# Dilated attention: another order of TensorE's work within a unit

## What is computed

```
qkv = einsum('bhwc,oc->bohw', x, Wqkv)          # q, k, v for 2 dilations (2 and 3), 64 channels each
kw, vw = unfold_windows(k, v, 3 x 3 taps, dilation)
attn = softmax(einsum('bndhw,bndkhw->bnkhw', q, kw) * 0.25, over the 9 taps)   # per head and position
out  = einsum('bnkhw,bndkhw->bndhw', attn, vw)
x    = x + concat(out) @ Wproj.T + bproj
```

## Time and profile before

| | |
|---|---|
| median of 3 runs | 7381.07 us (7369.02 to 7398.86) |
| profiled execution | 7399.85 us |
| its span, first to last instruction | 7397.9 us |
| mean granted clock of PE | 0.688 |
| PE busy | 3084.1 us, 42% |
| DVE busy | 3409.7 us, 46% |
| ACT busy | 1538.9 us, 21% |
| POOL busy | 2602.1 us, 35% |

### The profile page before, as it was taken

One profiled execution on the slowest core, in us unless ns is written; L12 is line 12 of the kernel. 1 busy time (PEld: TensorE's weight loads), 2 busy tenths in 40 slices (PEclk: granted clock), 3 DMA queues, 4 the chain that ended last, 5 costly groups with the idle time before them and its releaser, 6 DMA issues.

```text
span 7397.9 us, 84797 instructions
## 1 busy us (share of the span) xinstructions
PE 3084.1 (42%) x32140; PEld 1902.7 (26%) x32141; DVE 3409.7 (46%) x6941; ACT 1538.9 (21%) x3954; POOL 2602.1 (35%) x2472
## 2 busy tenths in 40 slices
PE   0011117687887798738874122222222222222205
PEld 0011106553773485226722000000000000000104
DVE  9999935757766685726665011111111111111128
ACT  0000005421651274016510011111111111111100
POOL 0000051100000000040001777777777777777450
PEclk9965558886997698658975555555565655555556
DMA  2000023000100100010002122222222222222207
GB/s 78 0 0 0 0 68 116 25 1 23 16 2 1 37 4 1 0 27 3 2 1 39 16 32 37 32 38 32 32 32 32 32 32 32 32 32 32 62 7 244
DMA packets 259708, 227.82 MB, mean 31 GB/s; under 512 B 115005, under 2 KB 222954, under 8 KB 250282
## 3 DMA queue, kind: packets, MB, share of 16 engines
q0 software_dynamic: 78944, 29.28, 6.3%
q1 hardware_dynamic: 99786, 99.91, 4.4%
q10 hardware_dynamic: 80640, 93.86, 4.1%
HBM read 100.42 MB, written 121.39 MB: 30 GB/s over the span
## 4 chain that ended last, share of the span: by engine, by line
PE 26%; another core or an unknown queue 23%; issue 18%; DVE 17%; DVEq 6%; ACT 4%; DMA 3%; POOL 2%; ACTq 1%; SPq 0%; POOLq 0%
DVE SA_ L1305 3%; PE PSB L382 2%; PE PSB L679 2%; DVE SA_ L1295 2%; PE PSB L1157 2%; PE PSB L661 2%; PE PSB L527 2%; PE PSB L352 2%; POOL VPAD L958 2%; DVEq L1386 1%; PE PSB L392 1%; DVE SA_ L583 1%; PE PSB L516 1%; PE PSB L366 1%
## 5 line engine op out<-in xcount | busy, mean ns | idle before, releaser
L948 POOL DMA_INDIRECT SA_<-s_T,GIX x2048 | 2186.6, 1068 | 659.0 <-issue 659.0
L1157 PE MATMUL PSB<-VPAD,EH 128*128 128x512 f32 x512 | 299.4, 748 | 1995.6 <-DMA VPAD<-s_TNT 1562.0
L940 POOL DMA_INDIRECT s_AEXP<-fill,SIX x128 | 139.2, 1087 | 2467.4 <-DMA fill<-s_ADT 2426.3
L897 DVE TENSOR_TENSOR XPAD<-SA_ 128x256 f32<-128x256 f32 x32 | 14.2, 444 | 1830.3 <-DMA SA_<-s_T,GIX 1830.3
L1157 PEld LDWEIGHTS PSB<-VPAD,EH 128*128 128x128 f32 x512 | 120.6, 245 | 2195.3 <-DMA VPAD<-s_TNT 1603.6
L1161 PE MATMUL PSB<-SA_,EW 128*128 128x512 f32 x512 | 346.3, 825 | 345.2 <-ACT SA_ L1142 198.6
L849 POOL DMA_INDIRECT SA_<-s_SK,BLKI x128 | 121.0, 945 | 1018.5 <-DVE BLKI L1438 976.9
L303 ACT ACTIVATE PRX<-PSB,MX 128x144 f32<-128x144 f32 x1024 | 375.3, 380 | 337.2 <-DVE MX L224 337.0
L1409 PE MATMUL PSB<-ident,SA_ 128*128 128x128 f32 x448 | 81.8, 364 | 838.0 <-DVE SA_ L1376 576.7
L1146 ACT ACTIVATE VPAD<-PSB,PRX 128x512 f32<-128x512 f32 x128 | 87.9, 687 | 1308.4 <-remote 941.7
L1142 ACT ACTIVATE SA_<-PSB,PRX 128x512 f32<-128x512 f32 x256 | 175.9, 687 | 773.7 <-remote 432.4
(11 more groups left out here) (365 smaller groups left out, 7536.3 us busy)
## 6 DMA issues: line engine op xcount, KB each, us to landing
SA_<-s_T,GIX POOLq DMA_INDIRECT x2048
s_Y<-VPAD ACTq DMA_DIRECT2D x32, 1024.0 KB
s_R<-zero SPq DMA_DIRECT2D x96, 256.0 KB
s_R<-XPAD ACTq DMA_DIRECT2D x32, 768.0 KB
SB_<-s_Y SPq DMA_DIRECT2D x16, 1024.0 KB, 5.4
SA_<-s_Y SPq DMA_DIRECT2D x16, 1024.0 KB, 7.3
s_AEXP<-zero SPq DMA_DIRECT2D x32, 256.0 KB, 3.0
SA_<-in_x SPq DMA_DIRECT2D x16, 512.0 KB
```

The costliest lines, as they stand in the source:

```text
L948: pool.indirect_dma_start(out=n.G[:,s,c,:],out_offset=None,in_=d["T"],in_offset=IOA(ap=n.GIX[s][:,c:c+1],axis=0)).then_inc(n.gath[s],16)
L1157: pe.matmul(PSB[:,(m%4)*512:(m%4+1)*512],n.WM1[:,m//2,(m%2)*P:(m%2+1)*P],n.TNC[:,s,:],start=True,stop=True).then_inc(n.moe_h,1)
```

## The change

In `l1conv_pe` the steps of a unit are put in another order. Before: head sums 0,1 of the next unit; expansions 0,1 and 2,3; the queries of the unit after the next; head sums 2,3 and 4,5; expansions 4,5; head sums 6,7,8. After: expansions 0,1; head sums 0,1; expansions 2,3; head sums 2,3; expansions 4,5; queries; head sums 4,5 and 6,7,8. The projection and expansions 6,7 and 8 follow as before. Nothing else is touched.

```
         turn_weights(m)
+        expand_pair(m,0)
         if more: logit_pair(m+1,0)
-        expand_pair(m,0); expand_pair(m,2)
+        expand_pair(m,2)
+        if more: logit_pair(m+1,2)
+        expand_pair(m,4)
         if m+2<UNITS: queries(m+2)
-        if more: logit_pair(m+1,2); logit_pair(m+1,4)
-        expand_pair(m,4)
+        if more: logit_pair(m+1,4)
         if more: logit_pair(m+1,6); logits(m+1,8)
         if closing: project(m//2-1,0)
         expand_pair(m,6)
```

## The result

| | before | after |
|---|---|---|
| median of 6 runs each | 7394.32 us (7369.02 to 7407.17) | 7452.75 us (7450.76 to 7455.88) |
| ratio | | 1.009, 95% interval 1.0074 to 1.0105 |
| span of the profiled execution | 7397.9 us | 7450.6 us |
| first to last softmax of the units, images 0, 1, 2, 3 | 170.0, 179.5, 179.5, 179.5 us | 191.2, 188.5, 188.5, 188.6 us |
| their sum | 708.4 us | 756.8 us |

The change made the kernel 0.9% slower. Of the 52.7 us by which the two spans differ, 48.3 are in the units of the dilated attention: 21.2 in image 0 and some 9 in each other image. So the loss is where the change is. The 4.4 us outside are within scatter: over the profiles of the twelve kernels of this document that rest lies between 6676.0 and 6700.7 us. From the first to the last softmax there are seven units, 0 to 6; unit 7, whose steps the change leaves alone, lies behind the last softmax.

What follows compares the result with a forecast made beforehand. No engine is full; stages have their own limits, here expansions 6,7 and the clock. Images 1 to 3 add 30.3 us, image 0 19.6: 49.9 on 7399.85 gives 7449.8, less half of 18.8: 7440 us, range 7390 to 7480.

Steps and rivals of the forecast that it cites:

- Step 1: Unit start: expansion 0 at 1.75 us instead of 2.86, value 0 gains 1.11 us, TensorE loses 0.68 uncovered.
- Steps 2 and 3: Steps laid end to end at 1.2 GHz put queries at 11.47 us; VectorE gains 1.25 us up to value 4.
- Step 4: Ordinary units: clock rises 2.66 to 4.66 us after the later queries, delaying expansions 6,7 and value 6; 1.6 us longer.
- Step 5: Units 2 and 4, which project before expansions 6,7: value 6 at 19.72 to 20.72 instead of 18.12, 2.1 us longer.
- Step 6: Unit 6, without queries: 1.05 us slower without a clock rise, some 2 gained with one; taken as minus 0.5.
- theory 3: Formed after four experiments, not forecast: the clock rises behind head sums and queries unbroken by expansions, which hold it down.
- (a): Rival, chance 0.20: clock rises at 11.4 us in the unit as before, queries or not; 7392 us, no change.
- (b): Rival, chance 0.10: alternating expansions and head sums lift the clock early, ordinary units 2.3 us shorter; 7332 us.
- (c): Rival, chance 0.15: clock rises late or falls soon, projections run at 1.2 GHz, value 6 at 24.74; 7486 or 7477 us.

Runs made afterwards that it cites:

- x2: The kernel before with the queries alone moved behind expansions 4,5: 7358.91 us, ratio to before 0.9972.
- x10: The changed kernel with head sums 4,5 moved ahead of expansions 4,5: 7383.34 us, ratio to before 0.9997.
- x4: The changed kernel with extra matmuls whose results nobody reads, where TensorE waits for a softmax: 7327.56 us, ratio to before 0.9927.
- x5: The kernel before with the extra matmuls of x4: 7343.5 us, ratio to before 0.9954.
- x3: The changed kernel with head sums 0,1 put back ahead of expansions 0,1: 7391.35 us, ratio to before 1.0020.
- x6: The kernel before with the queries moved to the start of the unit, behind the weight transposes: 7401.86 us, ratio to before 1.0030.
- x8: The kernel before with head sums 0,1 moved behind expansions 0 to 3: 7392.79 us, ratio to before 1.0015.
- x1: The changed kernel with the queries put back behind expansions 2,3: 7400.7 us, ratio to before 1.0027.

## Why the prediction was right, and where it was not

**What held.** The time (7452.75 in 7390 to 7480; the point forecast 7440) and its direction. Step 1: first expansions at 1.75, value 0 at 3.86, against 1.75 and 3.85. Steps 2 and 3: value 2 at 7.72 and value 4 at 11.58, against 7.71 and 11.57; the queries at 11.48 against 11.47. The walk over measured steps at one clock was good to 0.02 us.

**Step 4, the size.** The rise at 14.13 to 16.13 was forecast; image 1's units 0 to 5 have 13.8 to 16.7. Value 6 starts at 17.5 to 18.0 in units 1, 3 and 5 against 16.69 to 17.69: the high end and beyond, and so these units are 1.8 to 2.3 us longer, where I took 1.6; unit 0 is 1.4 longer. Step 5: value 6 at 20.02 and 19.77 in units 2 and 4, inside 19.72 to 20.72. Step 6: the clock did rise in unit 6, at 14.19, and it gained 2.0 us, where I took 0.5 between two cases. Image 0: plus 21.2 against 19.6. Images 1 to 3: plus 9.0, 9.0 and 9.1 against 10.1. These errors nearly cancel: the units' sum is 48.3 against 49.9. The point forecast is 13 us low mostly because it took 9.4 us, half of what lay between the profiled execution and the median, off the sum. Without that the sum is 7449.8, against 7452.57 for the profiled execution. The six runs of the changed kernel lie within 5.1 us, those of before within 38, which fits with the new order having lost the early rises altogether, but no second profile of before shows it.

**Step 4, the reason.** "Keeping the delays from queries to rise" gave the right times for a wrong cause. It took two units in which the rise came after queries and made the queries its origin. The trace of the kernel before already spoke against it: in image 0 the clock rose at 3.47, 3.75 and 3.53 us in units 0, 2 and 3, ahead of queries at 5.0 to 5.2, and at 3.74 in unit 6, which has none. The prediction saw unit 0 alone and set it aside as a special case. Unit 6 of the changed kernel, without queries too, rises at 14.2 to 14.3 in all images, and x2 settles it: the clock rises 1.5 us before the unit's first query. In the order of before and in the changed order the queries happened to open the first stretch without expansions, so the two readings gave the same number. That the time came out right was luck in this step. x10 tells the readings apart the other way round: later queries, earlier rise.

What stands in its place is this. The loss is the later rise: with the clock held up it is gone (x4, x5). One pair of head sums moved decides between a rise at 9.7 to 11.9 us (x10) and at 13.8 to 17.0 (the changed kernel), as theory 3 has it. That is not the only way back: x3 leaves head sums 2,3 and 4,5 apart and comes within 8 us of x10, by early rises in 13 of its 28 units. Why expansions differ from head sums for the clock (they read 32 partitions, head sums 128) no run here shows.

**What stays open.** How long such a run has to be, and what it takes beside it. Theory 3 is no law of the unit's own order. Unit 6 has no queries, so its steps are the same in the kernel before, in x2 and in x6. The clock rose in it at (us from its first transpose):

| | image 0 | image 1 | image 2 | image 3 |
|---|---|---|---|---|
| before | 3.74 | never | never | never |
| x2 | 8.95 | 3.84 | 10.92 | 11.06 |
| x6 | 9.35 | never | 9.12 | 9.07 |

In images 1 to 3 of the kernel before, four head sums in a row (3.56 us in image 1) lifted nothing, in x2 the same ones did, and in x8 a run of 7.3 us was hardly rewarded. In x1 23 of the 24 units 0 to 5 rise at 10.2 to 12.3 us and one at 15.90. So where a unit stands in time, or what the units ahead of it did, matters beside its order, and no run here isolates that.

**The rivals.** (a), the same rise at 11.4 us, did not happen in the change, but x8 and x10 are near that case: 7393 and 7383 us, against 7392. (b), the early rise, did not happen either. The nearest to it is x4, with help: 19.75 us per ordinary unit is 3.8 less than before, where (b) had 2.3 less with value 0 still at the low clock's 3.85; in x4 it starts at 2.47. In the changed kernel 15.0 us of busy TensorE in 15.7 stayed at 0.50, and in x4 the extra matmuls held 1.00. The Trainium skill, "TensorE: Matmul & The Clock Gate", section "What's actually happening", says that activity releases the throttle; x4 agrees with that, but being busy was not enough in the changed kernel. (c) was not seen: in image 1 the first projections of units 2 and 4 ran at the high clock, the units took 29.67 and 29.07 us, and in no image did value 6 of such a unit start later than 21.70, against the 24.74 of (c).

**The version that beats both kernels** is x4: 7327.56 us, 0.73% under before and 1.7% under the changed kernel. Without extra matmuls it is x2, 0.28% under before.

## What to carry to other kernels

When a stage's engines are all partly idle, read the granted clock of each stretch before moving matmuls: here the same steps in the same order took 19.75 or 25.45 us per unit, by the clock. An order can keep TensorE busy and slow at once; try matmuls of one kind in a row, and try filling the wait ahead of them. And when a rule is read off a trace ("it rises behind X"), look for one unit without X before building on it: here the trace of the kernel before had four.

## What the runs showed of the hardware that was not expected

- TensorE was at 1.2 GHz for 15.69 us of which it was busy for 15.01 (changed kernel, image 1, unit 3), and in unit 6 of the kernel before for all of 30.47 us with 28.16 busy. Busy time does not tell the clock.
- The clock can fall during unbroken work. In x4, unit 2 of image 1, TensorE was busy without a pause from the first expansion on when the clock fell, 13.93 us later, within the second projection:

```profile
2328.30:2342.23 13.93, 13.93 (x64) 4.93 (x64) 11.38 (x18) 1.19 (x2) 0.00 (x0) 1.00 0.00 0
```

- 17 extra matmuls per ordinary unit, 7.55 us at the high clock, made the kernel faster by 1.7% against the changed one: at that clock they fit into time in which TensorE waited. Behind a fall they do not, and push the next unit back (x5: 4.55 us).
